# Eight extra matmuls a slot on TensorE, in front of the maximum matmuls of steps 8 and 9

## What is computed

```
x = x + attention(layernorm(x))        # q = x W_q, k and v from a 32-wide latent, rope, causal softmax, W_o
x = x + cross_attention(layernorm(x))  # 8 heads of 64, 32 context rows, Wo, bo
x = x + ffn(layernorm(x))              # fp4(w_down) . fp4(silu(fp4 gate) * fp4 up)
```

## Time and profile before

| what | value |
|---|---|
| median of 3 runs | 439.47 us (438.8 to 440.79) |
| the profiled execution | 441.66 us, its span 439.9 us |
| TensorE matmul busy | 299.1 us, 68% |
| VectorE busy | 301.8 us, 69% |
| ScalarE busy | 177.1 us, 40% |
| GpSimd busy | 194.2 us, 44% |
| mean granted TensorE clock | 0.805 |
| idle of PE before L1070, ended by DVE L821 | 51.6 us |
| idle of DVE before L821, ended by PE L1070 | 50.5 us |

### The profile page before, as it was taken

One profiled execution on the slowest core, in us unless ns is written; L12 is line 12 of the kernel. 1 busy time (PEld: TensorE's weight loads), 2 busy tenths in 40 slices (PEclk: granted clock), 3 DMA queues, 4 the chain that ended last, 5 costly groups with the idle time before them and its releaser, 6 DMA issues.

```text
span 439.9 us, 6518 instructions
## 1 busy us (share of the span) xinstructions
PE 299.1 (68%) x1790; PEld 143.7 (33%) x1790; DVE 301.8 (69%) x1137; ACT 177.1 (40%) x327; POOL 194.2 (44%) x374
## 2 busy tenths in 40 slices
PE   1603675786696886859594959597777847666464
PEld 1301341332242222235342334334233424434243
DVE  5526858555656567689889787778777465687972
ACT  5410363754554535245465444344425413222110
POOL 4200234642214354354666553535445552745653
PEclk9999999977886559579887778687959779667796
DMA  6079000160300051004002600030000000000000
GB/s 182 0 213 195 1 1 2 58 161 1 73 3 0 12 183 26 0 1 80 1 7 72 152 1 7 1 79 1 9 6 3 7 0 7 6 1 7 1 13 18
DMA packets 20835, 17.50 MB, mean 40 GB/s; under 512 B 1920, under 2 KB 20224, under 8 KB 20800
## 3 DMA queue, kind: packets, MB, share of 16 engines
q1 hardware_dynamic: 20272, 16.50, 15.3%
q10 hardware_dynamic: 528, 0.59, 0.4%
HBM read 9.62 MB, written 7.34 MB: 39 GB/s over the span
## 4 chain that ended last, share of the span: by engine, by line
PE 46%; DVE 25%; issue 10%; POOL 7%; ACT 6%; DMA 4%; SPq 1%; POOLq 0%; DVEq 0%; ACTq 0%
PE pvp L1105 11%; PE mxp L1070 6%; PE st L1094 5%; DVE summed L821 4%; PE misc L1184 3%; PE misc L1166 2%; PE pvp L1116 2%; PE misc L1169 2%; PE mxp L1005 2%; DVE space L755 2%; ACT probs L622 2%; DMA ks<-parts_dram 2%; PE misc L1141 2%; DVE space L752 2%; POOL space L462 2%
## 5 line engine op out<-in xcount | busy, mean ns | idle before, releaser
L821 DVE CUSTOM_DVE_ANT_0 summed<-mxp,causal 128x512 bf16<-128x512 f32 (+3 forms) x256 | 114.2, 486 | 50.8 <-PE mxp L1070 50.5
L622 ACT ACTIVATE probs<-st 128x1024 f32<-128x1024 f32 (+1 forms) x96 | 84.5, 880 | 116.9 <-PE st L1094 116.7
L1070 PE MATMUL mxp<-ks,qs 48*128 48x512 bf16 (+3 forms) x256 | 43.3, 376 | 70.8 <-DVE rmax L821 51.6
L1105 PE MATMUL pvp<-probs,va 128*32 128x128 f32 (+3 forms) x512 | 63.3, 571 | 5.1 <-POOL probs L432 5.1
L432 POOL TENSOR_SCALAR_AFFINE_SELECT probs<-probs 128x256 f32<-128x256 f32 x128 | 48.1, 411 | 34.1 <-ACT probs L622 34.1
L1094 PE MATMUL st<-qs,ks 50*128 50x512 bf16 (+3 forms) x256 | 42.1, 369 | 7.1 <-ACT probs L622 5.7
L1070 PEld LDWEIGHTS mxp<-ks,qs 48*128 48x128 bf16 x256 | 12.2, 100 | 94.7 <-DVE rmax L821 45.7
L532 ACT ACTIVATE space<-misc 128x128 f32<-128x128 f32 (+3 forms) x78 | 24.2, 327 | 38.9 <-PE misc L1125 20.3
L423 POOL TENSOR_SCALAR var<-mv 128x1 f32<-128x1 f32 (+1 forms) x36 | 8.9, 248 | 54.1 <-DVE mv L728 52.7
L1094 PEld LDWEIGHTS st<-qs,ks 50*128 50x128 bf16 x256 | 12.2, 101 | 61.5 <-issue 42.3
L462 POOL TENSOR_TENSOR space<-space 128x128 f32<-128x128 f32 (+2 forms) x33 | 24.7, 748 | 15.1 <-DVE space L758 15.1
(11 more groups left out here) (196 smaller groups left out, 576.4 us busy)
## 6 DMA issues: line engine op xcount, KB each, us to landing
parts_dram<-parts SPq DMA_DIRECT2D x8, 384.0 KB, 2.6
qs<-parts_dram SPq DMA_DIRECT2D x16, 192.0 KB, 3.9
ks<-parts_dram SPq DMA_DIRECT2D x16, 192.0 KB, 4.5
parts_dram<-parts SPq DMA_DIRECT2D x8, 256.0 KB, 2.9
xin<-in_x SPq DMA_DIRECT2D x4, 256.0 KB, 6.0
parts_dram<-parts SPq DMA_DIRECT2D x8, 128.0 KB, 2.8
out<-outr SPq DMA_DIRECT2D x16, 64.0 KB, 1.6
qs<-nrows SPq DMA_DIRECT2D x32, 4.0 KB
```

The lines of the kernel that those rows point to most:

```text
L622: nc.scalar.activation(probs[n % 2][:, 2 * pair:2 * pair + 2, 512 * k:512 * k + w], st2[:, :].rearrange("p (h q) -> p h q", h=2)[:, :, 0:w ...
L821: last = v.tensor_tensor_reduce(out=summed[:, m % 2, e * w:(e + 1) * w], in0=mxp[m % 3][:, e * w:(e + 1) * w], in1=causal[:, S - w:S], sca ...
L1070: last = mm(units[r][:, e * w:(e + 1) * w], qs[rows, c, i * P:(i + 1) * P], ks[rows, c, 0:w], start=True, stop=True)
L1105: last = mm(pvp[32 * i:32 * i + 32, j * P:S], va[:, j, GH * (n % NG) + i, :], probs[n % 2][:, i, OFF[j]:OFF[j] + S - P * j], start=(j == 0 ...
```

## The change

A function `keep_busy` puts four matmuls of a bfloat16 128x128 identity with the 128x512 mask constant into the two score banks, alternating. It is called at steps 8 and 9, ahead of the maximum pair, in every slot n for which slot n+2 exists: slots 0 to 13, 112 matmuls in all. It first waits for the exponential of score unit 5 of its own slot (`probs_d` at 6n+6), the last reader of the banks; score unit 0 of the next slot overwrites what it wrote. Nobody reads the results.

```diff
+FILL_STEPS, FILLERS = [8, 9], 4
...
+            def keep_busy(n):
+
+                wait(pe, "probs_d", 6 * n + 6)
+                for i in range(FILLERS):
+                    mm(stp[i % 2], identb[:, :], causal[:, :], start=True, stop=True)
+
             def score_unit(n, u):
...
                     if (n, u) in SET_UP:
                         set_up(SET_UP.index((n, u)))
+                    if u in FILL_STEPS and in_range(n + 2):
+                        keep_busy(n)
                     for ahead, p in PAIR_STEPS[u]:
                         if in_range(n + 1 + ahead):
                             max_pair(n + 1 + ahead, p)
```

## The result

| | before | after |
|---|---|---|
| median | 439.13 us (4 runs, 438.34 to 440.79) | 444.03 us (4 runs, 443.31 to 444.23) |
| ratio | | 1.0104, interval 1.0071 to 1.0136 |
| profiled execution | 441.66 us, span 439.9 | 443.31 us, span 441.6 |
| mean granted TensorE clock | 0.805 | 0.817 |

The changed kernel is slower; it was run a second time among the experiments, on another chip, with 1.008 (1.0057 to 1.0103). A ratio leaves out the runs that lie more than 1.5% above the fastest of the same kernel, a median keeps them. So sums of stretches from these traces explain the 1.7 us and not the whole of the 4.9.

What follows compares the result with a forecast made beforehand. Bound: a chain alternating between VectorE and TensorE, its dense TensorE stretch run at half clock behind quiet stretches. Direct costs 9.8 us less clock gains 12.3 give -2.5 us: 437.0 us against the median of 439.47, range 428 to 447.

Steps and rivals of the forecast that it cites:

- it cancels: Rival, chance 0.20: clock falls in step 0 of every late slot, 4.7 us of gain vanish; 439.5 to 441.7 us.
- the fall merely moves: Rival, chance 0.20: clock falls at the dense stretch's start, low as long; only 1.6 us gained against 9.8, 447.5 us.
- clock up: Rival, chance 0.20: clock stays up through whole late slots; 21.6 us gained against 9.8, about 427.5 us.
- So a fall moved behind step 9 is worth 0.47 us: Late slots: a later clock fall shortens a slot from 20.77 us, as in slot 11, to slot 12's 20.30.
- the gain of 1.6 us: Sum for later falls: 0.47 us each in slots 10, 11 and 13, about 0.2 in slot 7.
- 2.4 us of cost and 6.3 of gain: Slots 7 to 13: direct cost of blocks against 1.6 us from later falls and 4.7 from the clock staying up.
- 7.35 of cost and 6 of gain: Slots 0 to 6: direct cost of blocks against clock gains of 4 us in slots 2 and 3, 2 in slot 5.
- The clock stays up: Slots 7 to 13: dense stretch at full clock saves about 2.0 us, in one slot of three: 4.7 us.
- The direct costs: Delay from blocks at steps 8 and 9, slots 0 to 13: 0.9 us a block at full clock, 9.8 us summed.
- the 1.1 named: Sign: a block's four fillers take about 0.9 us at full clock; over 1.1, slots 7, 10, 11 and 13 lose too.
- the sign named for the forecast: Mean granted clock above 0.805, near 0.86; over 0.92 would mean clock up, near 0.81 a fall that only moves.
- the two signs of being wrong: Clock falling ahead of pair 1 despite the blocks, or low time longer than before because it begins with the dense stretch.

Runs made afterwards that it cites:

- e9_again: The changed kernel unaltered, run again on another chip beside other follow-ups: 445.02 us over 12 runs, ratio 1.008 to the kernel before.
- e10: Changed kernel with blocks of steps 8 and 9 only in slots 7 to 13, plus a block at step 0 of slots 8 to 14: 431.42 us, 0.9785.
- e5: Changed kernel with both blocks only in slots 0 to 6: 438.84 us, ratio 0.9946 to the kernel before.
- e3: Changed kernel with both blocks only in slots 7 to 13: 442.10 us, ratio 1.0029 to the kernel before.
- e12: Changed kernel with only step 9's block, only in slots 7 to 13: 440.52 us over 12 runs, ratio 0.9877 to the kernel before.
- e2: Changed kernel with only the block of step 9, step 8's removed: 437.16 us, ratio 0.9859 to the kernel before.
- e4: Changed kernel plus a third block at step 0 of slots 8 to 14, ahead of pair 2: 431.25 us, ratio 0.9728 to the kernel before.
- e1: Changed kernel with the wait for the exponential kept and the filler matmuls removed: 444.91 us, ratio 1.006 to the kernel before.

## Why the prediction was wrong

437.0 us was forecast, 444.03 measured: inside the range, but slower where faster was the likeliest. The change of 4.9 us lies between those of two rivals, "it cancels" (2.2 us) and the one in which the fall merely moves (9.8 - 1.6 = 8.2 us; on the median of 439.47 that is 447.7 and not the 447.5 of the prediction, and "clock up" 427.7).

**The failed step** is "So a fall moved behind step 9 is worth 0.47 us", with the gain of 1.6 us built on it, and the comparison in the earlier trace rows on which it rests. I set slot 12 (20.30 us) against slot 11 (20.77) as a late fall against an early one. But they differ in two more things. The low time was 6.6 us in slot 12 and 10 in slot 11, and the work isn't the same: at full clock throughout, stretch 12 takes 19.1 us after and stretch 10, with slot 11's work, 18.2. The traces after keep the slot and change the fall. With the late fall and 10.1 us of low time slots 11 and 13 took 22.0 us, 1.2 us more than before. In the second trace (e9_again) the clock fell in step 0 too, some 2 us sooner (pair 2 of slot 11, at 284.08, takes 0.50 us there instead of 0.34), with 6.9 us of low time, and they took 20.3:

```profile
275.99:296.28 20.29, 16.93 (x106) 7.73 (x106) 16.04 (x63) 8.56 (x17) 9.50 (x20) 0.83 0.24 44
...
316.86:337.19 20.33, 16.97 (x106) 7.73 (x106) 16.04 (x63) 8.55 (x17) 9.49 (x20) 0.83 0.02 4
```

So what shortens the stretch is a shorter low time. A fall that moves behind step 9 and stays as long costs 1.2 us where the prediction had a gain of 0.47.

Cutting stretch 11 at the start of pair 2 shows where. Before, then after:

```profile
273.67:282.39 8.72, 4.32 (x31) 2.12 (x31) 7.01 (x24) 3.21 (x6) 4.15 (x7) 0.77 0.01 2
282.39:294.45 12.06, 11.70 (x70) 5.25 (x70) 9.04 (x40) 5.24 (x11) 5.34 (x14) 0.74 0.35 72
```

```profile
273.80:281.88 8.08, 5.31 (x38) 2.47 (x38) 6.99 (x24) 3.31 (x6) 4.15 (x7) 1.00 0.01 4
281.88:295.83 13.95, 13.22 (x69) 5.45 (x70) 9.06 (x40) 5.24 (x11) 5.34 (x14) 0.63 0.31 61
```

Ahead of pair 2 the late fall gains 0.64 us, since pair 1, the transposes and score unit 0 run at full clock. Behind it it loses 1.89 us. e10, without low time, takes 10.09 us for that second part, so its low time of 6.3 us before cost 1.97 us and the 10.3 us after cost 3.86: about 0.3 to 0.4 us for each us of low time. The 4 us of low time ahead of pair 2 cost 0.64, about 0.16 for each, with 1.86 us of idle in them; in the 10 us of low time after only 0.73 us was idle.

**The size of it.** For slots 7 to 13 the prediction has 2.4 us of cost and 6.3 of gain, -3.9 us. Their stretches came out at +2.9 and +3.1 us in two traces: a miss of 7 us, the largest of all. In after's trace the five stretches in which the clock fell (7, 8, 9, 11 and 13) sum to +6.8 us, the two in which it stayed up to -3.8. For slots 0 to 6 the prediction has 7.35 of cost and 6 of gain, +1.35 us. There the traces after are 1.4 to 1.7 us shorter than before's, and e5 by itself gains 2.4 us; but the unfilled early slots of other kernels vary by more than that between traces (125.1 us in e3, 128.8 in e12), so the sign there rests on e5's interval alone.

**The clock stays up.** "One slot in three" was sized well for the profiled execution (stretches 10 and 12 of seven) and "2.0 us" each too low for stretch 10, which gained 2.6 us, and too high for 12 with 1.2. But no late stretch stayed up in e9_again's trace, and one in e3's: 3 in 21, and 3.8 us where there were two. Its counterpart was left out: a slot in which the clock doesn't stay up was priced as a gain of 0.47 and is a loss of up to 2.9. The rival "it cancels" had the fall in step 0 in every late slot, e9_again's case, and went wrong at the same 1.6 us. The rival "the fall merely moves" named the right mechanism, but it too counted the 1.6 us as a gain. Its test, that the low time between 77 and 335 us be no less than before, was wrong: by the mean clock of that stretch (0.76 before, 0.88 after, 0.87 in e9_again) it fell from some 124 us to some 62 and 67, and the kernel was still slower.

**What the transposes do.** The Trainium skill, "TensorE: Matmul & The Clock Gate" (Part 4: PE-mode transpose), has transposes not counting as activity for the clock as other matmuls do. In this trace the clock fell in step 0, behind L1123 and the wait for pair 2, in four of the seven late slots (7, 8, 11, 13), and in slot 9 for the second time, which fits; in slots 10 and 12 it held over the same transposes. No run separates the transposes from the idle time around them.

**The direct costs** were right or nearly so:

- A block at full clock was put at 0.9 us and took 0.97, at the low clock at 1.75 and took 1.84 (64.53 to 66.37, below). That is close to what the rows of the same type gave, and far from the float32 bound of 2.0.
- Slot 3: forecast 1.25 us. The timeline below has the exponential's end at 115.17 and VectorE's unit 0 at 116.62, 1.45 us behind it; before it was 0.09 (114.82, 114.91 in the earlier trace rows), so 1.36 us. By e2 against after, 1.2.
- Slot 0: forecast 1.7 at the low clock, measured 1.7 (24.9 against 23.2). In e4's trace the clock was up for these blocks already, and stretch 0 took 23.7 us, 0.5 more than before. Slot 6: forecast 1.65, measured 2.0 at equal low time (21.6 against 19.6). Slot 11: forecast hidden, and hidden.
- Slot 2 was mis-sized: 0.3 forecast, 1.5 measured (e2 against after). The block does lie under the wait for the DMA, as read, but the transfer itself is late: in the row below pair 0 still waits 0.63 us for it behind the block, and starts 3.51 us into the stretch (103.14 - 99.63), in e2 2.00 (100.13 - 98.13). What is late at its source I did not settle. Slot 12: 1.1 forecast, 0.4 measured (19.1 against 18.7 of e2, both without low time).
- The wait by itself (e1) costs 2.6 us. The prediction had it inside the blocks' costs and didn't price it apart.

The timeline after, of slot 0, slot 2 and slot 3, and of e2 in slot 2:

```profile
64.53 1.91 PE L1088 MATMUL st<-causal,identb 128*128 128x512 bf16 x4
66.37 0.61 PE L1071 MATMUL mxp<-ks,qs 48*128 48x512 bf16 x2
...
103.14 0.39 PE L1071 MATMUL mxp<-ks,qs 48*128 48x512 bf16 x2 [0.63 <-DMA ks<-parts_dram]
```

```profile
100.13 0.39 PE L1071 MATMUL mxp<-ks,qs 48*128 48x512 bf16 x2 [1.18 <-DMA ks<-parts_dram]
```

```profile
114.60 0.57 ACT L623 ACTIVATE probs<-st 128x512 f32<-128x512 f32 x1
...
116.19 0.39 PE L1071 MATMUL mxp<-ks,qs 48*128 48x512 bf16 x2
...
116.62 0.69 DVE L822 CUSTOM_DVE_ANT_0 summed<-mxp,causal 128x512 bf16<-128x512 f32 x1 [3.65 <-PE mxp L1071]
```

**The signs named ahead.** The four fillers took 0.97 us, under the 1.1 named. The transposes took 0.66 us in six of the late slots, but 1.11 in slot 9. The mean clock came out at 0.817, which looks like the 0.81 named for the moving fall but isn't: after's record holds the low time from 24 to 69 us that before's lacks. Left out, it would be about 0.87 (an estimate: 0.817 + 0.5 x 44.4 / 441.6). So the sign named for the forecast came, and the time didn't follow. The low stretches began behind step 9, save one of slot 9's (below): there the clock fell ahead of pair 1 in spite of the blocks, one of the two signs of being wrong. The other, "a fall whose low time is longer than before because it begins with the dense stretch", has the right place. In slots 8, 11 and 13 the low time was not longer, only fuller; in slot 9, with two falls, it was longer too.

**What stays open.** Why the early and the late blocks together cost 4.6 to 5.7 us more than the sum of each alone. That one slot's clock depends on where it fell in the slot before, so that parts of such a change needn't add, is a guess that no run here tests. By the times, the late blocks alone are not slower than before beyond the interval of e3; that late stretches with both blocks lose about 3 us rests on three traces (150.6, 150.8 and 151.0 us) against two without (147.7 both). Whether step 9 alone helps the late slots (e12) is open as well.

## What to carry to other kernels

When filling quiet places ahead of dense work to keep the clock up, look at which of them stays open: here two blocks a slot ahead of an open wait cost 1%, and a third, directly in front of the dense work, turned the same kernel into one 2.7% faster than the one without fill. One block alone, at step 9 or at step 0, gained 1.3 to 1.4%, while one in front of work that another engine was waiting for lost 1.2%. Judge low clock by what is busy in it, with a window over the low time itself, not by its length or the mean clock of the run. And a comparison of two slots is worth a term of the sum only if one thing differs between them.

## What the runs showed of the hardware that was not expected

- The clock can fall while a block of fillers runs. In slot 9 after, the first block came behind 1.78 us of idle, and the second took 1.73 us instead of 1.03, its end and all behind it at the low clock:

```profile
234.18 1.04 PE L1088 MATMUL st<-causal,identb 128*128 128x512 bf16 x4 [1.78 <-ACT probs L623]
...
235.64 1.73 PE L1088 MATMUL st<-causal,identb 128*128 128x512 bf16 x4
...
237.84 1.11 PE L1123 MATMUL pvp<-ident,oT 128*128 128x128 f32 x4
```

- The mean granted clock of a run can lack the low time at its start, as shown in the section on the result. The runs of one kernel then fall in two groups: the changed kernel's in e9_again lie at 0.809 to 0.813 and at 0.856 to 0.863, with times of 443.5 to 443.9 and 442.3 to 445.9 us. The distance of some 0.05 is what the 44 us of low time from 24 to 69 us are worth in 442. Before's runs lie in two groups too, at 0.733 to 0.750 and at 0.790 to 0.815. So a difference of 0.05 between two runs tells nothing until both records are seen to begin at the same time.
- The spread of runs differs much between these kernels: before 6 us over 23 runs, e2 12 over 6, e12 13 over 12, the changed kernel in e9_again 17 over 12. Why was not tested.
